# Kernel of four layers on one core: last layer's low parts moved behind its sums, its first products earlier, its gates into its loop

## The reference

```python
x = x + _L1_attn_ref(_layernorm(x, axis=-1), L1_attn_w_qkv, L1_attn_w_out)
x = x + _L1_ffn_ref(_layernorm(x, axis=-1), ...)

def _L1_ffn_ref(x, gate_w, bias, up_w, up_b, down_w, down_b, sw_up, sb_up, sw_down, sb_down):
    scores = jax.nn.sigmoid(xf @ gate_w + bias)                      # 8 experts
    top_scores, top_idx = jax.lax.top_k(scores, 2)
    top_scores = top_scores / (jnp.sum(top_scores, axis=-1, keepdims=True) + 1e-06)
    w = jnp.zeros((T, E)).at[jnp.arange(T)[:, None], top_idx].add(top_scores)
    hact = jax.nn.gelu(jnp.einsum('th,ehi->tei', xf, up_w) + up_b, approximate=False)
    eo = jnp.einsum('tei,eih->teh', hact, down_w) + down_b
    combined = jnp.einsum('teh,te->th', eo * 0.1, w)
    shared = (jax.nn.gelu(xf @ sw_up + sb_up, approximate=False) @ sw_down + sb_down) * 0.1
    out = (shared + combined).reshape(b, s, h)
    return out / (jnp.max(jnp.abs(out), axis=-1, keepdims=True) + 1e-06)
```

## Time and profile before

| | us |
|---|---|
| median of 3 runs | 1197.3 |
| their range | 1196.84 to 1199.27 |
| the profiled execution, its own time | 1198.93 |
| its span, first to last instruction | 1197.3 |
| TensorE busy in the span | 1064.8 (89%) |
| VectorE, ScalarE, GpSimd busy | 900.9 (75%), 714.3 (60%), 400.5 (33%) |
| the last phase, from its first transposition | from 949.9 on |

### The profile page before, as it was taken

One profiled execution on the slowest core, in us unless ns is written; L12 is line 12 of the kernel. 1 busy time (PEld: TensorE's weight loads), 2 busy tenths in 40 slices (PEclk: granted clock), 3 DMA queues, 4 the chain that ended last, 5 costly groups with the idle time before them and its releaser, 6 DMA issues. The chain is left out here.

```text
span 1197.3 us, 18618 instructions
## 1 busy us (share of the span) xinstructions
PE 1064.8 (89%) x6893; PEld 552.9 (46%) x6893; DVE 900.9 (75%) x1573; ACT 714.3 (60%) x1216; POOL 400.5 (33%) x254
## 2 busy tenths in 40 slices
PE   5379859999999999999788999999999769899996
PEld 3256655455545455555412222222212347688885
DVE  7958577866666667667677999999997246888777
ACT  5323536443344454433267888888888678588874
POOL 1137501767677776777512200000010011122200
PEclk9559989999999999999969999999999979899998
DMA  4000010000000000100011111010010102633521
GB/s 95 1 1 3 1 36 1 1 10 2 1 1 2 2 2 1 54 28 1 1 44 32 36 41 28 15 27 15 15 20 1 37 1 43 97 74 69 73 36 35
DMA packets 46017, 29.35 MB, mean 25 GB/s; under 512 B 10784, under 2 KB 42664, under 8 KB 45928
## 3 DMA queue, kind: packets, MB, share of 16 engines
q1 hardware_dynamic: 45928, 28.17, 11.0%
HBM read 23.57 MB, written 4.26 MB: 23 GB/s over the span
## 5 line engine op out<-in xcount | busy, mean ns | idle before, releaser
L1997 ACT ACTIVATE narrow_att_probs<-psum 128x512 f32<-128x512 f32 x512 | 264.9, 603 | 61.7 <-PE psum L1922 61.5
L2017 DVE TENSOR_REDUCE front_maxima<-psum 128x1 f32<-128x1024 f32 x240 | 281.9, 1219 | 19.9 <-PE psum L1031 15.5
L1276 POOL TENSOR_TENSOR gated_tally<-gated_probs,gated_tally 128x1024 f32<-128x1024 f32 x96 | 230.9, 2405 | 77.6 <-ACT gated_probs L1535 69.1
L1535 ACT ACTIVATE gated_probs<-psum 128x1024 f32<-128x1024 f32 x128 | 124.1, 1021 | 159.4 <-PE psum L1423 156.8
L1637 DVE TENSOR_REDUCE gated_maxima<-psum 128x1 f32<-128x512 f32 x256 | 164.6, 685 | 50.2 <-PE psum L1313 49.0
L1922 PE MATMUL psum<-narrow_att_q,narrow_att_k 50*128 50x512 bf16 x448 | 146.0, 384 | 5.9 <-ACT narrow_att_probs L1997 5.4
L1031 PE MATMUL psum<-narrow_att_k,narrow_att_q 48*128 48x512 bf16 x448 | 132.6, 381 | 11.2 <-DVE front_maxima L2017 2.5
L1935 PE MATMUL psum<-narrow_att_probs,narrow_att_v_ones 128*32 128x512 f32 x1024 | 138.1, 612 | 0.1
L2429 DVE TENSOR_TENSOR moe_hidden_lo<-moe_hidden,moe_hidden_hi 128x512 fp32r<-128x512 f32 x144 | 99.5, 717 | 44.4 <-ACT moe_hidden_hi L2351 44.0
L1436 PE MATMUL psum<-gated_probs,gated_values 128*64 128x512 f32 x512 | 132.1, 610 | 0.0
L2347 ACT ACTIVATE moe_hidden<-psum,back_up_bias 128x512 f32<-128x512 f32 x144 | 96.1, 689 | 41.6 <-PE psum L73 41.5
(11 more groups left out here) (384 smaller groups left out, 1930.8 us busy)
## 6 DMA issues: line engine op xcount, KB each, us to landing
moe_mixb<-moe_mix_scratch SPq DMA_DIRECT2D x8, 1024.0 KB, 15.7
narrow_parts_scratch<-gated_values SPq DMA_DIRECT2D x12, 128.0 KB, 2.1
narrow_parts_scratch<-narrow_att_part SPq DMA_DIRECT2D x12, 128.0 KB, 2.2
narrow_att_q<-narrow_parts_scratch SPq DMA_DIRECT2D x14, 96.0 KB
narrow_att_q<-narrow_parts_scratch SPq DMA_DIRECT2D x42, 32.0 KB
narrow_att_k<-narrow_parts_scratch SPq DMA_DIRECT2D x14, 96.0 KB
narrow_att_k<-narrow_parts_scratch SPq DMA_DIRECT2D x42, 32.0 KB
X<-in_L_attn_inputs SPq DMA_DIRECT2D x4, 256.0 KB, 3.9
```

Source lines behind the costliest of these rows:

```text
L1276: pool.tensor_tensor(tally[:, n % 2, :, :], probs[:, kt % 4, :, :], so_far, ALU.add).then_inc(tallied, 1)
L1535: act.activation(probs[:, k % 4, :, :], psum[:, 2 * e:2 * e + 2, :], ACT.Exp, scale=SCALE).then_inc(exped, 1)
L1997: act.activation(probs[:, k % 3, 2 * e + u % 2, :], psum[:, SCORE_BANK + j % 3, :], ACT.Exp, scale=SCALE).then_inc(exped, 1)
L2017: dve.tensor_reduce(maxima[:, n % 2, at:at + 1], chunk.rearrange("p a b -> p (a b)"), AX.X, ALU.max).then_inc(chunk_used, 1)
```

## The change

It writes the work of the phase in another order; no product is dropped or added.

- `turn` gets `bank=4`: the transposed quarters go into banks 4 to 7, so that `up` can write banks 0 to 3 while the later quarters are still turned. For that `down(0)` and `down(1)`, which write banks 6 and 7, wait for the third and the fourth low part.
- TensorE turns three quarters, does `up(0)` after the first low part, turns the fourth, and goes on with `up(1)`, `down(0)`. The gate logits come after `up(2)`, the scores' transposition after `down(1)` (`GATES_AT = 2`).
- ScalarE loads the Sqrt table by a small instruction ahead of the roots; it does the fourth high part behind step 0 and the sigmoid behind step 1. The Gelu table is loaded twice, ahead of step 0 and again behind the sigmoid.
- VectorE does `add_results(3)` ahead of the first low part, the fourth low part behind step 0, and the four parts of the choice two and two in steps 2 and 3, where they stood one each in steps 0 to 3.
- GpSimd starts the split of the first expert's weights on the fourth low part, not on the logits.
- SyncE waits until the first broadcast has landed, and loads the third expert's weights then.

The diff, its blank lines left out:

```diff
--- before.py
+++ after.py
@@ -2138,10 +2138,10 @@
         AH, AL = (w[:, :, :, :].rearrange("p k a t -> p (k a t)")[:, 0:TOK] for w in (hidden_hi, hidden_lo))
-        shift = ph.sb("shift", [P, TILES])
+        shift, table = ph.sb("shift", [P, TILES]), ph.sb("table", [P, 1])
         norm = Norm(ph, "norm", X, U)
         results = Turn(ph, "results", psum, C["ident"], lambda t: back.attended[:, t, :], AH, AL, None)
-        turn = Turn(ph, "turn", psum, C["ident"], lambda t: U[:, t, :], UH, UL, None)
+        turn = Turn(ph, "turn", psum, C["ident"], lambda t: U[:, t, :], UH, UL, None, bank=4)
         projected, added, shift_ready = ph.sem("projected"), ph.sem("added"), ph.sem("shift_ready")
         small_loaded, up_loaded, down_loaded = back.small_loaded, back.up_loaded, back.down_loaded
         up_hi_ready, up_ready = back.up_hi_ready, back.up_ready
@@ -2164,7 +2164,7 @@
         acc_turned = ph.sem("acc_turned")
         peak_step = ph.sem("peak_step")
         result_ready = ph.sem("result_ready")
-        GATE_STEPS, MIX_AT = 10, 4
+        GATE_STEPS, GATES_AT, MIX_AT = 10, 2, 4
         def up_src(e):
             return io["L1_ffn_up_w"][e] if e < E else io["L1_ffn_sw_up"]
@@ -2201,6 +2201,8 @@
             sp.wait_ge(mix_stored, 16)
             for n in range(1, ALLE):
                 mixb_load(sp, n)
+                if n == 1:
+                    sp.wait_ge(mixb_loaded[1], 16)
                 if n + 2 < ALLE:
                     weights_load(n + 2)
             for q in range(QUARTERS):
@@ -2214,7 +2216,7 @@
             for n in range(1, ALLE):
                 pool.wait_ge(up_loaded[n % 2], 16 * (n // 2 + 1))
                 if n == 1:
-                    pool.wait_ge(logits_done, 1)
+                    pool.wait_ge(turn.lo_ready, QUARTERS)
                 else:
                     pool.wait_ge(up_done, (n - 1) * QUARTERS * FB)
                 pool.tensor_copy(up_hi[n % 2][:, :], raw_up[n % 2][:, :]).then_inc(up_hi_ready, 1)
@@ -2260,16 +2262,21 @@
                     t = q * PER_Q + i
                     last = split_product(pe, psum[:, 4 + q, tile(i)], AH[:, tile(t)], AL[:, tile(t)], front.wo_hi[:, :], front.wo_lo[:, :])
                 last.then_inc(projected, 1)
-            for q in range(QUARTERS):
+
+            def turn_quarter(q):
                 pe.wait_ge(norm.normed, (q + 1) * PER_Q)
                 for i in range(PER_Q):
-                    last = pe.transpose(psum[:, q, tile(i)], turn.view(q * PER_Q + i), C["ident"])
+                    last = pe.transpose(psum[:, 4 + q, tile(i)], turn.view(q * PER_Q + i), C["ident"])
                 last.then_inc(turn.turned, 1)
-            gate_logits()
+
+            for q in range(QUARTERS - 1):
+                turn_quarter(q)
             def up(n, q):
                 if q == 0:
                     pe.wait_ge(up_ready, n + 1)
+                if n == 0:
+                    pe.wait_ge(turn.lo_ready, q + 1)
                 for a in range(FB):
                     k = (n * QUARTERS + q) * FB + a
                     if k >= 4:
@@ -2282,7 +2289,10 @@
                 k = n * QUARTERS + q
                 if q == 0:
                     pe.wait_ge(down_ready, n + 1)
-                if k >= 2:
+                if k < 2:
+
+                    pe.wait_ge(turn.lo_ready, 3 + k)
+                else:
                     pe.wait_ge(term_ready, k - 1)
                 for a in range(FB):
                     pe.wait_ge(hidden_lo_ready, k * FB + a + 1)
@@ -2304,11 +2314,15 @@
             for k, (n, q) in enumerate(steps):
                 up(n, q)
                 if k == 0:
-                    turn_scores()
+                    turn_quarter(QUARTERS - 1)
+                if k == GATES_AT:
+                    gate_logits()
                 if k == MIX_AT:
                     turn_mix()
                 if k >= 1:
                     down(*steps[k - 1])
+                if k == GATES_AT:
+                    turn_scores()
                 if k - 2 >= (ALLE - 1) * QUARTERS:
                     turn_back((k - 2) % QUARTERS)
             down(*steps[-1])
@@ -2325,14 +2339,13 @@
             for q in range(QUARTERS):
                 results.quarter_high(act, q)
+            act.wait_ge(norm.eps_ready, 1)
+            act.activation(table[:, :], norm.eps[:, :], ACT.Sqrt)
             for q in range(QUARTERS):
                 norm.quarter_root(act, q)
                 apply(q)
                 if q >= 1:
                     turn.quarter_high(act, q - 1)
-            turn.quarter_high(act, QUARTERS - 1)
-            act.wait_ge(logits_done, 1)
-            act.activation(scores_t[:, :], psum[:, 4, :], ACT.Sigmoid, bias=back.gate_bias[:, 0:1]).then_inc(sigmoid_done, 1)
             for n in range(ALLE):
                 e = (n + E) % ALLE
                 for q in range(QUARTERS):
@@ -2350,6 +2363,11 @@
                             act.wait_ge(hidden_ready, k * FB + a)
                             act.activation(hidden_hi[:, k % 2, a - 1, :], hidden[:, k % 2, a - 1, :],
                                            ACT.Copy).then_inc(hidden_hi_ready, 1)
+                    if k == 0:
+                        turn.quarter_high(act, QUARTERS - 1)
+                    if k == GATES_AT - 1:
+                        act.wait_ge(logits_done, 1)
+                        act.activation(scores_t[:, :], psum[:, 4, :], ACT.Sigmoid, bias=back.gate_bias[:, 0:1]).then_inc(sigmoid_done, 1)
                     if k == MIX_AT:
                         act.wait_ge(mix_turned, 1)
                         act.activation(mixw_t[:, :], psum[:, 5, 0:P], ACT.Copy).then_inc(mix_copied, 1)
@@ -2379,13 +2397,12 @@
             center(0)
             add_results(2)
             center(1)
+            add_results(3)
             turn.quarter_low(dve, 0)
-            add_results(3)
             center(2)
             turn.quarter_low(dve, 1)
             center(3)
             turn.quarter_low(dve, 2)
-            turn.quarter_low(dve, 3)
             def choose_step(k):
@@ -2468,8 +2485,11 @@
             for k in range(ALLE * QUARTERS):
                 low_parts(k)
-                if k < MIX_AT:
-                    choose_step(k)
+                if k == 0:
+                    turn.quarter_low(dve, QUARTERS - 1)
+                if k in (MIX_AT - 2, MIX_AT - 1):
+                    for step in range(2):
+                        choose_step(2 * (k - MIX_AT + 2) + step)
                 if k >= 1:
                     add_term(k - 1)
             finish(0)
```

## The result

The changed kernel takes 1194.93 us where the kernel before takes 1198.12 in the same comparison (medians of 20 runs each). The ratio is 0.9977, 95% interval 0.9969 to 0.9986: 2.8 us less, between 1.7 and 3.7. Against the 1197.3 us from which the forecast was worked out that is 1194.5; forecast were 1193.8 and a range of 1191.6 to 1197.0. The profiled execution took 1195.64 us (span 1194.0).

The account below looks back on a forecast made before the run. The kernel's end was taken to hang on when the gates are transposed (`turn_mix`) and what follows; -1.4 (resumption), -2.0 (clock) and -0.1 gave -3.5 us, 1193.8 from 1197.3; own range 1192.8 to 1195.2, 8 in 10 1191.6 to 1197.0.

Parts of the forecast that it names:

- The start moves 8.0 us ahead: Head of the last phase: the first Gelu starts at 969.7 instead of 977.71 us.
- Gates on the path: Steps 0 to 2: gate matmuls take 1.7 us, done at 981.2; step 2's Gelus start at 983.4.
- The choice bunches up: VectorE, steps 2 and 3: 10.9 us of dense work from 988.6; TensorE waits over 6 us in `turn_mix`.
- GpSimd gets in the way: Second expert's split beside VectorE's choice: holds up last low part and first large comparison, 1.5 us; `turn_mix` at 1000.9.
- From `turn_mix` to the landing: Copy of the mix gains 1.0 us, store 1.54, broadcast 15.2; landing at 1018.4 against 1018.46, nothing gained.
- The resumption: TensorE goes on behind the first broadcast's landing, in step 6, at 1020.6 instead of 1022.05, 1.4 us gained.
- The third split's meeting: Third expert's split beside low parts behind the broadcast: put at no cost, meeting ones TensorE wants 2 us later.
- The clock: Falls in the `turn_mix` wait, about ten slow matmuls, 2.1 us hidden in the broadcast; `down(6)` at full clock, 2.0 gained.
- The meeting at the choice: Its rival: the second expert's split misses VectorE's choice, all behind 1.5 us earlier, -5.0 us, 1192.3; 20%.
- The table switch: Rival at ScalarE's table loads ahead of steps 0 and 2: each costs 1.4 us more, -0.7 us, 1196.6; 4%.
- the second broadcast: Rival: held back, it becomes the bound from a landing of 1040.8 on; up to 2.5 us slower, 1199.8; 7%.
- the short wait: Hole ahead of `down(6)`, 0.7 us; late-clock rival: clock falls at the start or here again (+2.0), -1.5 us, 1195.8; 17%.

Follow-up runs that it names:

- e5: Changed kernel with gate matmuls ahead of step 2's first products, scores' transposition ahead of `down(1)`, and VectorE's choice ahead of the same step's low parts: ratio 0.9935.
- e3: Changed kernel with GpSimd's split of the second expert's weights held until the choice is done: ratio 0.9965 to the kernel before.
- e2: Changed kernel without SyncE's wait for the first broadcast, so the third expert's weights load right behind it: ratio 0.9978 to the kernel before.
- e4: Changed kernel with GpSimd's split of the third expert's weights held until `down(6)` is done: ratio 0.9959 to the kernel before.
- e9: Changed kernel with the swap at the head undone, the first low part again ahead of `add_results(3)`: ratio 0.9980 to the kernel before.
- e12: Changed kernel with the head's swap undone and the third expert's split held behind step 6's low parts: ratio 0.9978 to the kernel before.
- e6: Changed kernel with the first broadcast cut into four DMAs, each with its own semaphore: ratio 0.9973 to the kernel before.
- e11: Changed kernel with the second expert's split held behind the choice and the third's behind step 6's low parts: ratio 0.9952 to the kernel before.
- e1: Kernel before with one edit, `add_results(3)` ahead of the first low part: ratio 0.9979 to the kernel before.
- e8: Kernel before with only the first broadcast cut into four DMAs, nothing holding the next loads back: ratio 0.9947 to the kernel before.

## Why the prediction was right, and where it was off

The time lies in the range and the sign is right, and the chain ran as forecast up to TensorE's resumption; the loss inside `down(6)` was not foreseen. By its own steps:

- **The start moves 8.0 us ahead**: shown. The first Gelu is 8.13 us earlier from the fixed point: 15.97 us behind it, where 969.7 less 953.61, 16.1, was forecast.
- **Gates on the path**: shown. They took 1.9 us instead of 1.7, from 978.92; step 2's Gelus start at 982.91, forecast 983.4, so from the fixed point 0.2 later than forecast.
- **The choice bunches up**: shown. `turn_mix` is 47.28 us behind the fixed point, forecast 1000.9 less 953.61, 47.29. TensorE's wait is 7.35 us. e5 shows that the order of work makes it, and not the amount: the same instructions one block earlier leave none of it.
- **GpSimd gets in the way**: shown by e3, 1.23 us where I took 1.5. The bounds were 0 and 2.6. It fell otherwise than I had it: the last low part lost nothing (the cast at 987.54 waited itself, 1.15 us), and the second comparison lost 1.10, not the first. The Trainium skill (page "SBUF — State Buffer", section "Who interferes with whom") has a VectorE instruction with two inputs in SBUF contend with a GpSimd instruction that reads SBUF. The traces agree: the second comparison took 2.32 us beside the split, and 1.22 in e3, where the split was away.
- **From `turn_mix` to the landing**: the copy follows faster, as forecast. The broadcast took 14.68 us instead of 15.2. Whether that is the wait's doing is open: e2, without it, took 14.5.
- **The resumption** was forecast 66.99 us behind the fixed point (1020.6) and came at 66.65 (1019.61): it follows the first term by 2.23 us, where it was 3.59 before, so the 1.4 us are there; the rest is mostly the faster broadcast.
- **The third split's meeting is the mis-sized term**: I put it at nothing, since its weights would land "some 3 us after the broadcast" and meet low parts "that TensorE wants 2 us later". They landed 2.6 us after their issue, and step 6's low parts lost 1.50 us. `down(6)`, for which I counted 2.8 us, took 4.03; step 8 began at 70.68 instead of 69.8. e4, with the split moved away, gives what the term holds: `down(6)` takes 2.79 us, the end comes 1.18 earlier. How large the meeting is hangs on small shifts: in e9 the low parts lost 0.41 us. Forecast for the edit were -3.5 us, measured are -2.65 in the traces. The timed runs (1.7 to 3.7 less) do not tell these two apart, and part of the closeness is luck: TensorE resumed 0.3 us earlier than forecast, and the meeting cost 1.2 us more.
- **The clock**: behind `turn_mix` six matmuls and not ten ran at the lower clock, hidden in the broadcast either way. That is why the wait ahead of `down(6)` was 1.20 us and not 0.7: TensorE came there earlier. Behind nearly the same wait of 7.35 to 7.40 us it was twelve in e2 and e4, ten in e12, eight in e9 and seven in e6, so the 2.1 us of the forecast needed a spread. `down(6)` runs at the full clock, as forecast. The two windows show the fall and its end:

```profile
998.00:1000.00 2.00, 0.00 (x0) 0.00 (x0) 1.83 (x6) 0.00 (x0) 0.00 (x0) 0.50 0.00 0
...
1004.00:1006.00 2.00, 2.00 (x10) 1.66 (x9) 0.75 (x1) 0.56 (x1) 1.15 (x2) 1.00 0.45 89
```

- **The rivals.** The meeting at the choice did happen. The table switch cost its load and no more: sigmoid at 980.91 for 0.69, load at 981.61 for 1.28, Gelu at 982.91. The Trainium skill (page "ScalarE: Activation LUTs", section "What ACT_TABLE_LOAD costs") counts a drain of about 1.38 us beside the load; this row shows none. No term waited for the second broadcast. The clock did not fall again in the short wait.

The forecast did not ask which part of the change carries the gain. The swap at the head alone gives 0.9979. The gates among the steps bring the first Gelu 6.6 us further ahead (15.97 against 22.61) and put `turn_mix` 2.66 us later than that swap alone. That both come out alike is due to the copy of the mix, which no longer stands behind high parts, a slightly faster broadcast, a first low part that no split holds up, and `down(6)` at the full clock.

## What to carry to other kernels

When a long transfer is waited for, ask first what its first reader needs: the first quarter of this broadcast was there 9 us before the whole would have been, and this one cut gave over twice what the change gave (0.9947 against 0.9977). The better order of e5 gave as much (0.9935), and both together 0.9880. Work moved out of the way of the start must not come later on the chain that sets the end: the same gates and choice, one block earlier, turned a gain of 3 us into one of 8. And where GpSimd splits weights beside VectorE, the split's start belongs behind the step that others wait for; one wait on a semaphore did it, for 1.50 and 1.18 us at the end of the traces.

## What the runs showed of the hardware

- A waiting GpSimd instruction got ahead of VectorE's next one. The subtraction at 988.76 took 2.16 us, 0.87 over its usual 1.29, and ended at 990.92. If it ran for its usual time it ran from 989.63, when the first comparison was ending. The second comparison then took 2.32 us, 1.10 more than the 1.22 without a split (e3). VectorE had its three comparisons queued densely and still lost its turn.
- The first broadcast of 1 MB took 14.4 to 14.7 us in the seven traces in which the next loads were held back (after, e3, e4, e5, e9, e11, e12), and 15.32, 15.06 and 14.5 us in the three with two loads of weights issued behind it (before, e1, e2). Three traces do not tell whether the loads cost it anything.
- A load of 256 KB landed 2.6 us after its issue with nothing ahead of it in the queue (issue at 1017.30, cast at 1019.90). Two of them landed 13.9 and 12.8 us after theirs with four quarters of the broadcast ahead of them (e8).
- With one and the same wait of 7.35 us ahead of it, six matmuls ran at the lower clock in one trace (after) and twelve in two others (e2, e4).
